# A four-layer graph network on one core: setup reordered by its loads, scaling of the first layer's rows moved into the end of the count stage, and one maximum over partitions taken with TensorE

## What is computed

```python
x = _layernorm(x + _L0_gnn_ref(x, edge_index, L0_gnn_gamma), axis=-1)
x = _layernorm(x + _L1_gnn_ref(x, L1_gnn_qW, L1_gnn_kW, L1_gnn_vW, src, dst), axis=-1)
x = _layernorm(x + _L2_gnn_ref(x, L2_gnn_weights, L2_gnn_loop_w, L2_gnn_bias, src, dst, edge_type_8), axis=-1)
x = _layernorm(x + _L3_gnn_ref(x, L3_gnn_W0, L3_gnn_b0, L3_gnn_W1, L3_gnn_b1, L3_gnn_W2, L3_gnn_b2, src, dst), axis=-1)
```

```python
def _L0_gnn_ref(x, edge_index, gamma):          # ten steps of normalised propagation
    deg = jax.ops.segment_sum(jnp.ones((src.shape[0],), x.dtype), dst, num_segments=n)
    dinv = jnp.where(deg > 0, jax.lax.rsqrt(jnp.maximum(deg, 1.0)), 0.0).astype(x.dtype)
    norm = (dinv[src] * dinv[dst])[:, None]
    out = gamma[0] * x
    h = x
    for k in range(STEPS):
        h = jax.ops.segment_sum(h[src] * norm, dst, num_segments=n)
        out = out + gamma[k + 1] * h
    return out

def _L1_gnn_ref(embeds, qW, kW, vW, rows, cols): # attention over the edges, 4 heads
    q, k, v = (embeds[rows] @ qW), (embeds[cols] @ kW), (embeds[cols] @ vW)
    scores = jnp.clip(jnp.einsum('ehd,ehd->eh', q, k), -10.0, 10.0)
    ...
```

## Time and profile before

| | |
|---|---|
| median of 3 runs | 3117.41 us (3113.38 to 3125.9) |
| the profiled execution | 3099.45 us, of which the span is 3097.7 us |
| its mean granted TensorE clock | 0.872 of full speed |
| PE busy | 2500.3 us (81%) |
| DVE busy | 2208.7 us (71%) |
| ACT busy | 1219.7 us (39%) |
| POOL busy | 525.3 us (17%) |
| setup | 0 to 49.7 us of the span |
| counts | 49.7 to 525.7 us |
| preparation of the first layer | 525.7 to 542.4 us |
| first layer | 542.4 to 1088.9 us |
| preparation of the attention layer | 1088.9 to 1111.4 us |

### The profile page before, as it was taken

How to read it: one execution, slowest core, us unless ns; L and a number is a source line. 1 busy time by engine, 2 the same in 40 slices (tenths; PEclk the granted TensorE clock), 3 DMA queues, 4 the chain that set the end, 5 groups by cost and what they waited for, 6 DMA issues and landing times. The chain is left out here.

```text
span 3097.7 us, 63262 instructions
## 1 busy us (share of the span) xinstructions
PE 2500.3 (81%) x21707; PEld 1816.3 (59%) x21708; DVE 2208.7 (71%) x4679; ACT 1219.7 (39%) x2267; POOL 525.3 (17%) x919
## 2 busy tenths in 40 slices
PE   3999996999999967877776767777785877777687
PEld 1555553999999921111112466677663767766687
DVE  7999998555656569999998555566663656665545
ACT  2888886322333259999996300000021000000212
POOL 1111111000000000000000434433315243334000
PEclk8999998999999978888886878888796888877698
DMA  2333332111110041111112412112143111112510
GB/s 67 132 127 130 130 147 109 44 34 34 33 34 33 2 118 38 37 36 37 37 37 71 149 40 54 44 49 53 41 101 101 48 44 51 51 51 34 225 45 17
DMA packets 94360, 206.47 MB, mean 67 GB/s; under 512 B 21958, under 2 KB 60358, under 8 KB 94050
## 3 DMA queue, kind: packets, MB, share of 16 engines
q1 hardware_dynamic: 80290, 182.46, 17.0%
q0 software_dynamic: 13888, 21.36, 4.2%
HBM read 118.17 MB, written 84.76 MB: 66 GB/s over the span
## 5 line engine op out<-in xcount | busy, mean ns | idle before, releaser
L1738 PE MATMUL l_bank<-tab,mask 128*128 128x192 f16 x7600 | 786.9, 264 | 277.5 <-issue 268.0
L1738 PEld LDWEIGHTS l_bank<-tab,mask 128*128 128x128 f16 x7600 | 692.4, 105 | 367.8 <-issue 356.7
L1315 DVE TENSOR_SCALAR mask<-code 128x1600 int32<-128x1600 int32 x304 | 546.4, 1816 | 440.3 <-remote 352.4
L743 PE MATMUL sums<-u,ct 128*128 128x192 f16 x6250 | 526.7, 248 | 31.0 <-PEq L726 22.1
L743 PEld LDWEIGHTS sums<-u,ct 128*128 128x128 f16 x6250 | 522.4, 99 | 34.8 <-PEq L726 22.2
L1710 POOL DMA_INDIRECT ggot<-table_dram,gidx x432 | 410.3, 950 | 148.8 <-issue 124.1
L1189 DVE SCALAR_TENSOR_TENSOR pr<-ex,cring 128x1568 f32<-128x1568 f32 x200 | 356.0, 1780 | 6.3 <-ACT ex L1159 4.7
L1115 PE MATMUL score<-qa,ka 96*128 (+1 forms) x800 | 236.0, 397 | 137.7 <-DVE least L1182 112.1
L1115 PEld LDWEIGHTS score<-qa,ka 96*128 96x128 f16 x800 | 55.8, 104 | 379.8 <-DVE least L1182 166.3
L372 DVE TENSOR_SCALAR hot<-iota,col 128x400 bf16<-128x400 f16 x1000 | 249.6, 314 | 0.0
L367 DVE TENSOR_SCALAR codehot<-iota,sel 128x128 bf16<-128x128 f16 x1000 | 240.3, 306 | 4.5 <-POOL sel L349 1.9
(11 more groups left out here) (303 smaller groups left out, 2558.2 us busy)
## 6 DMA issues: line engine op xcount, KB each, us to landing
code<-code_dram SPq DMA_DIRECT2D x38, 800.0 KB, 4.3
code_dram<-flat SPq DMA_DIRECT2D x100, 200.0 KB, 1.9
ct_dram<-ct SPq DMA_DIRECT2D x25, 800.0 KB, 3.6
c_dram<-flat SPq DMA_DIRECT2D x25, 800.0 KB, 3.4
ct_again<-ct_dram SPq DMA_DIRECT2D x25, 800.0 KB, 22.5
cring<-c_dram SPq DMA_DIRECT2D x200, 98.0 KB, 1.9
table_dram<-tab SPq DMA_DIRECT2D x50, 384.0 KB, 2.3
flat<-code_dram SPq DMA_DIRECT2D x19, 800.0 KB, 4.4
```

The costliest lines, as they stand in the source:

```text
L743: mm = e.matmul(sums[t % RS][:, 0:2 * D], ct[:, t, s, :], u[par][:, s, :, :].rearrange("p k d -> p (k d)"), start=(s == 0), stop=(s == NT ...
L1315: e.tensor_scalar(turned.rearrange("p (s q d) -> p s q d", q=NQ, d=DQ // 2), words.rearrange("p (q s d) -> p s q d", q=NQ, d=DQ // 2), abs ...
L1738: mm = e.matmul(acc[k][:, 0:2 * D], mask[:, r % MR, s, :], tab[:, s, r, :], start=(r == 0 and s == 0), stop=(r == R - 1 and s == NT - 1))
```

## The change

Four things are done.

1. Setup. SP issues `dst_em`, `src_em`, `typ_em` first and `dst_cm` last, each with a semaphore of its own; `x` and gamma are loaded here too, once `dst_cm` is in. DVE does the ten edge operations first and the wide ones after `dst_cm`; it waits for three of POOL's operations, not 13, and POOL does those three first. PE transposes the first half of `best` while DVE works on the second, and L234's reduction is split in two. The largest |x| of each partition is taken in five reductions of 480 elements. Nine tiny operations of `gather_tab` move on to the counts.
2. Counts. At the start, the largest |x| over partitions is taken by a PE transpose, a DVE reduction and a matmul with a row of ones. The last of the 25 tiles is taken out of the loops of DVE and ACT. Before it, DVE works out the degrees of tiles 0 to 22, and after it the scale, the scaled rows and their f16 parts, for tiles 0 to 22, then 23, then 24 (`PARTS`); ACT takes the square roots in between. SP no longer waits here for the stores to land.
3. The block of preparation is gone. What is left of it (`gd`, `x` times gamma[0]) stands at the start of DVE's program in the first layer, and SP's waits for the stores at the start of SP's.
4. In the preparation of the attention layer, the maximum over partitions is a PE transpose after the first projection matmul, a DVE reduction and a diagonal, and a matmul with ones after the second.

Tiles are placed anew: `codehot`, `hot` and `u[0]` share one tensor `onehots`; `edge_col`, `edge_sv` and `val` share `edges`.

The diff, cut to its core: first the tiles and the setup.

```diff
+        onehots = sb("onehots", [P, 2 * GRP * (P + WC)], BF16)
+        u = [onehots[:, 0:NT * 2 * D].bitcast(F16).rearrange("p (t k d) -> p t k d", k=2, d=D)]
...
-                    e.dma_start(src_em[:], a["src_em"]).then_inc(s_in, 16)
-                    e.dma_start(dst_em[:], a["dst_em"]).then_inc(s_in, 16)
-                    e.dma_start(typ_em, a["typ_em"]).then_inc(s_in, 16)
...
+                    e.dma_start(dst_em[:], a["dst_em"]).then_inc(s_dst, 16)
+                    e.dma_start(src_em[:], a["src_em"]).then_inc(s_src, 16)
+                    e.dma_start(typ_em, a["typ_em"]).then_inc(s_typ, 16)
...
+                    e.wait_ge(s_in, 16)
+                    e.dma_start(x[:], a["x_pt"]).then_inc(s_x_in, 16)
+                    e.dma_start(gam[:], a["gamma"].partition_broadcast(P)).then_inc(s_x_in, 16)
                     e.wait_ge(s_edge, 1)
+                    e.wait_ge(s_pool, MARGINS)
...
-                    e.wait_ge(s_in, 64)
-                    e.wait_ge(s_pool, 13)
+                    e.wait_ge(s_dst, 16)
...
+                    e.wait_ge(s_src, 16)
...
+                    e.wait_ge(s_typ, 16)
...
+                    e.wait_ge(s_in, 16)
                     c(e.tensor_reduce(cmm[:, :, 0], dst_cm, AX_X, ALU.min))
                     c(e.tensor_reduce(cmm[:, :, 1], dst_cm, AX_X, ALU.max))
+                    e.wait_ge(s_pool, 3)
...
+                    e.wait_ge(s_pe, 1)
+                    c(e.tensor_reduce(mb[:, 0, :], turned[:, 0, :, 0:QROW], AX_X, ALU.max))
+                    e.wait_ge(s_x_in, 32)
+                    largest(0)
                     e.wait_ge(s_pe, 2)
-                    c(e.tensor_reduce(mb[:], turned[:, :, :, 0:QROW], AX_X, ALU.max))
+                    c(e.tensor_reduce(mb[:, 1, :], turned[:, 1, :, 0:QROW], AX_X, ALU.max))
...
+                    for g in range(1, NT // 5):
+                        largest(g)
+                    c(e.tensor_reduce(xpart[:, 5:6], xpart[:, 0:5], AX_X, ALU.max))
```

```diff
+                    e.wait_ge(s_xt, 1)
+                    e.tensor_reduce(xone[:], counts[0:1, 2, 0:P], AX_X, ALU.max).then_inc(s_xone, 1)
...
+                    def degrees(i):
+                        ts = PARTS[i]
+                        e.wait_ge(s_turn_out, NR * ts.stop + 2)
+                        c(e.tensor_reduce(deg[:, ts], dacc[:, ts, :], AX_X, ALU.add))
+                        c(e.tensor_scalar(dinv[:, ts], deg[:, ts], 1.0, None, ALU.max))
+                        c(e.tensor_scalar(some[:, ts], deg[:, ts], 1.0, None, ALU.min))
+                        e.reciprocal(rdeg[:, ts], dinv[:, ts]).then_inc(s_sq, 1)
...
+                    def rows_scaled(i):
+                        ts = PARTS[i]
+                        e.wait_ge(s_sqo, i + 1)
+                        c(e.tensor_tensor(dinv[:, ts], dinv[:, ts], some[:, ts], ALU.mult))
+                        c(e.scalar_tensor_tensor(val[:, ts, :], x[:, ts, :], scale[:, 0:1],
+                                                 dinv[:, ts].unsqueeze(2).to_broadcast([P, ts.stop - ts.start, D]), ALU.mult, ALU.mult))
...
+                    def rows_split(i):
+                        ts = PARTS[i]
+                        c(e.tensor_copy(u[0][:, ts, 0, :], val[:, ts, :]))
+                        c(e.tensor_tensor(u[0][:, ts, 1, :], val[:, ts, :], u[0][:, ts, 0, :], ALU.subtract))
...
+                    with e.Fori(0, NT - 1) as t:
+                        tile(t)
+                    degrees(0)
+                    tile(NT - 1)
...
+                    power_of_two(c, e, power[:], xall[:], scale[:, 0:1])
+                    c(e.tensor_scalar(scale[:, 1:2], power[:], 2.0 ** -14, None, ALU.mult))
+                    rows_scaled(0)
+                    e.wait_ge(s_used, e.snap(n) + 1)
+                    rows_split(0)
+                    degrees(1)
...
+                    rows_scaled(1)
+                    rows_split(1)
+                    degrees(2)
+                    rows_scaled(2)
+                    rows_split(2)
```

PE, then ACT, then SP, in the counts:

```diff
+                    e.transpose(counts[0:1, 2, 0:P], xpart[:, 5:6], ident[:]).then_inc(s_xt, 1)
+                    e.wait_ge(s_xone, 1)
+                    e.matmul(codes[:, 2, 0:1], ones[:], xone[:], start=True, stop=True).then_inc(s_xall, 1)
...
+                    e.wait_ge(s_xall, 1)
+                    e.activation(xall[:], codes[:, 2, 0:1], ACT.Copy).then_inc(s_xread, 1)
...
-                    with e.Fori(2, NT) as t:
+                    with e.Fori(2, NT - 1) as t:
                         tile(t, False, False)
+
+                    def root(i):
+                        e.wait_ge(s_sq, i + 1)
+                        e.activation(dinv[:, PARTS[i]], rdeg[:, PARTS[i]], ACT.Sqrt).then_inc(s_sqo, 1)
+
+                    root(0)
+                    tile(NT - 1, False, False)
                     window_out(NT - 1, WPT - 1, n, False)
                     for q in range(NR):
                         row_out(NT - 1, q, False)
+                        if q == 0:
+                            root(1)
+                    root(2)
...
-                    e.wait_ge(s_row_out, 16 * NT)
-                    e.wait_ge(s_ct_out, 16 * NT)
-                    for k in range(2):
-                        e.wait_ge(s_stored[k], 32 * NT)
-                    e.wait_ge(s_x_in, 16)
+                    e.wait_ge(s_gtab, 1)
+                    e.dma_start(gather_tab[:], gi[:, :]).then_inc(s_gtab_in, 16)
```

```diff
-                        e.wait_ge(s_max, 2)
-                        e.partition_all_reduce(wall[:], wmax[:], P, bass.bass_isa.ReduceOp.max).then_inc(s_all, 1)
...
+                        e.wait_ge(s_wt, 1)
+                        c(e.tensor_reduce(wboth[:, 0:1], w_t, AX_X, ALU.max))
+                        e.tensor_scalar(wboth[:, 1:3], ident[0:2, 0:2], wboth[:, 0:1], None, ALU.mult).then_inc(s_diag, 1)
                         e.wait_ge(s_all, 1)
 
-                        c(e.tensor_scalar(wall[:], wall[:], float(D), None, ALU.mult))
+                        c(e.tensor_scalar(wall[:], w_p, float(D), None, ALU.mult))
...
+                                if n == 0:
+                                    e.wait_ge(s_max, 2)
+                                    e.transpose(w_t, wmax[:], ident[:]).then_inc(s_wt, 1)
+                                if n == 1:
+                                    e.wait_ge(s_diag, 1)
+                                    e.wait_ge(s_z, 2)
+                                    e.matmul(w_p, one2[:], wboth[:, 1:3], start=True, stop=True).then_inc(s_all, 1)
```

186 lines of the change are left out of this document (90 added, 96 removed).

## The result

| | before | after |
|---|---|---|
| median | 3121.26 us of 12 runs (3113.38 to 3126.72) | 3109.17 us of 12 runs (3100.95 to 3115.33) |
| the profiled execution | 3099.45 us | 3115.33 us |

The ratio is 0.9961 with a 95% interval of 0.9947 to 0.9975: 12.1 us faster, 7.7 us less than the 19.8 of the forecast, and the forecast median of 3097.6 us (range 3087 to 3109) was missed. The kernel before, run nine times more, came out 4 us slower than the median that the forecast had started from; against 3121.3 the same sum of -19.8 would have given 3101.5, still 8 us too low. The gain is real, though under the 0.5% that the forecast had called faster. The forecast held that a difference this small can't be told from none with this kernel; with 12 runs of each, 0.39% can.

The account below looks back on a forecast made before the run. DVE, nearly with PE, bounds the counts; setup is one DVE chain, and 29.1 us idle precede the first layer. -8.1 + 2.5 - 15.0 + 0.8 = -19.8 us gives 3079.6 profiled, 3097.6 median; range 3087 to 3109.

Parts of the forecast that it names:

- Setup: Before the counts: edge operations start on early data, `largest` and tiny operations shrink; next stage at 41.7 instead of 49.78, -8.1 us.
- Rival (3): Setup: edge arrays land in one lump at about 12 us, edge operations stay on the path; +7, 3104.6 us, chance 0.12.
- Counts' start: Transpose, reduction, matmul and ACT's copy before the first window, about 1.2 us, hidden behind POOL's start; 0, bound +1.
- Last tile taken out: Counts: DVE waits for tile 22's row sums, then does four operations; nothing absorbs this, +2.5 us, bounds 2.2 and 4.5.
- Tail: From last one-hot to first layer: stores' landing, barrier and all-reduce go; H+14.1 instead of H+29.1, -15.0 us, bounds -16.4 and -12.
- First layer: `gd` and `x` before DVE's first sum take about 5 us, covered by PE's five banks and DVE's free time: 0.
- Attention preparation: Maximum by PE starts ACT 1.9 us later, about half caught up before the scores: +0.8 us, bounds -0.3 and +1.9.
- Rivals (1) and (2): ACT table loads: (1) reload in each last-tile loop, 3104 us, chance 0.08; (2) double hold per switch, 3100.6 us, 0.12.
- Rival (4): Counts: one-hots slower in their new tensor, 10 ns more each is +20 us; 3120 us at the least, chance 0.05.
- POOL's first use: 3.3 us of first use of POOL's custom operation might move to the last layer; POOL idle ahead of it, taken 0.

Follow-up runs that it names:

- cm_first: The changed kernel with the load of `dst_cm` issued first again, the other three behind it; count stage starts at 47.55 us, setup 47.6 against 40.6.

## Why the forecast was wrong, point by point

The median lies 0.2 us outside the stated range, and the sum is 8.0 us off by stretches: attention preparation 4.0, counts 2.6, first layer 1.4, tail 1.1, and 1.1 the other way in setup.

- **Setup, -8.1: right, measured -9.2.** `dst_em` landed at 4.1 (forecast 4.8), the wide operations started at 11.24 (12.3), the counts at 40.62 (41.7). That one array lay on a quarter of the engines was read rightly from one row; cm_first shows that the order carries three quarters of the gain. `dst_cm` was in by 11.17 (12.1). Rival (3), the data wait, is what cm_first built, and is false for the change.
- **Counts' start, 0, bound +1: +0.5 at most.** The first `codehot` is 2.58 us after the stage's start, against 2.12 before. The counts without the last tile taken out are still 465.5 on the mean, 1.3 above before; the other 0.8 is spread or not found.
- **Last tile taken out, +2.5, bounds 2.2 to 4.5: mis-sized, +3.6.** DVE's gap of 2.77 is as worked out. The step that failed is "DVE is full and PE waits for it, so nothing absorbs this": it prices the gap alone. PE, which waited 2.93 us, was at half clock for 3.2 us soon after, and there DVE waited for PE. The forecast had priced a colder clock at the first layer, where the row stood, and not here.
- **Tail, -15.0: -13.9.** One term failed: the cast of 2208 elements was taken at the rate of a row with 806, 1.35 us, and took 2.45, its upper bound. The rest was within 0.2 us. The cast stood in the stated bounds, and the bound came true for a reason that the forecast did not have: the odd number of tiles. What the sum did not ask is what the tail would be without the last tile taken out: 13.3.
- **First layer, 0: +1.4**, not settled.
- **Attention preparation, +0.8, bounds -0.3 to +1.9: the largest miss, +4.8.** Two steps failed. ACT came 2.7 us later relative to the layer's start, where 1.9 had been worked out: the wait behind the second slow projection was in the sum, but the transposition took 0.42 us (0.2 to 0.3 taken) and the matmul with ones 0.58 (some 0.15 taken), so that the maximum was out 3.7 us after PE's first work instead of 3.1, and PE itself began 0.2 us later. The larger step is "PE at full clock 0.7, so about half is caught up": it took the clock's rise from the trace of before, and in the new order it came 8.6 us later, so nothing was caught up and 2.1 us more were lost.
- **Rivals (1) and (2), the table loads: false.** Two loads in the counts, one at each first use; no load stands between the square root and the next Sign. The drain that "ScalarE: Activation LUTs" of the Trainium skill (What ACT_TABLE_LOAD costs) adds to a load is shown by no run here. **Rival (4): false**, `hot` takes 0.25 us an operation as before.
- **POOL's first use.** The forecast took 0 for a first use that might move to the last layer. The 0 is right, the picture is not: the last layer had its own in the kernel before too, 15.3 us ahead of need, so nothing moved there. And the cost is not the 3.3 us of DVE's wait but 5.6 to 5.8 us of POOL from its change of configuration.

## What to carry to other kernels

Before work is put into the middle of a stage that PE and another engine fill together, price the pause twice: once as the gap, once as the clock that PE may lose by it; behind the stage the same work may cost less. Taking out a custom POOL operation can leave its first-use cost to the next one, and keeping one costs little if its first use stands 6 us ahead of need. Matmuls without use, put in to keep the clock up, gained 3.4 us in one place and cost in another where they did not even run: measure each by itself. In a setup, issue the array that lies on few DMA engines last.

## What the runs showed of the hardware

- PE's granted clock stayed at 0.50 for 11.8 to 13.2 us of unbroken work in seven traces of seven with the two small matmuls between the first projections, and for 4.0 to 6.9 us in four with projections alone.
- A cast f32 to f16 took 0.66 ns an element over 12 tiles and 1.19 over 11.
- POOL's select on 128x128 took 2.71 us beside DVE's operations with two inputs (2.87 each) and the cast behind it 2.83, each ending 0.14 us after DVE's; with DVE idle, in the trace of before, they took 0.29 each. It held nobody up, since DVE's operations kept their 2.87. "SBUF — State Buffer" of the Trainium skill (Who interferes with whom) has the port that the two share, and the traces agree.
- The kernel before took 2680 us on some chips and 3105 to 3123 on others, 425 to 443 us apart. Between one trace of either kind 270 us of that are PE's idle time and 151 its busy time in the third layer's matmuls.
- With 14 unused matmuls in the program ahead of the first layer, PE's second pause at each turn of that layer's loop came after 5 matmuls and took 1.8 to 2.6 us; without them it came after 14 or 16 and took at most 1.7.
